# A new border between two stages: five comparisons for a recurrence, two projection banks, and constants made elsewhere

## What is computed

```python
xn = layernorm(x)
q, k, v = xn @ Wq.T, xn @ Wk.T, xn @ Wv.T           # 16 heads of 32
attn = softmax(q k^T * 512**-0.5) + bias[s - t]      # relative bias after softmax
s = layernorm(attn @ v) * gamma + beta
h = square(relu(xn @ W_fc.T))                        # 2048 wide
y = h @ W_proj.T
mem, count = 0, 0
for _ in range(5):                                   # leaky integrate and fire
    mem = 0.9 * mem + y - (mem > 1)
    count += (mem > 1)
out = x + s * silu(count / 5)
```

## Time and profile before

| | |
|---|---|
| median of three runs | 3676.3 us (3675.13 to 3678.26) |
| the profiled execution | 3674.0 us |
| span of the profiled execution | 3672.2 us |
| PE busy | 3474.0 us, 95% |
| DVE busy | 2733.0 us, 74% |
| ACT busy | 2623.7 us, 71% |
| POOL busy | 1575.7 us, 43% |
| DMA moved | 260.90 MB, mean 71 GB/s |

### The profile page before, as it was taken

One profiled execution on the slowest core, in us unless ns is written; L12 is line 12 of the kernel. 1 busy time (PEld: TensorE's weight loads), 2 busy tenths in 40 slices (PEclk: granted clock), 3 DMA queues, 4 the chain that ended last, 5 costly groups with the idle time before them and its releaser, 6 DMA issues.

```text
span 3672.2 us, 55309 instructions
## 1 busy us (share of the span) xinstructions
PE 3474.0 (95%) x20204; PEld 1475.0 (40%) x20204; DVE 2733.0 (74%) x4090; ACT 2623.7 (71%) x3917; POOL 1575.7 (43%) x898
## 2 busy tenths in 40 slices
PE   3999999999999998799999999999999999999985
PEld 1444444444444443334334343343343433434331
DVE  5366666666766667877787887887888888788786
ACT  4233333333333332799999999999999999999994
POOL 1000000000000000266777778677776777777867
PEclk6999999999999999899999999999999999999997
DMA  4011111111111111313223133232232222323221
GB/s 174 30 42 41 42 41 41 41 42 41 50 62 41 41 41 35 92 42 92 76 81 117 59 92 105 76 112 69 86 111 76 87 93 82 93 84 90 82 76 64
DMA packets 141405, 260.90 MB, mean 71 GB/s; under 512 B 19248, under 2 KB 52784, under 8 KB 140624
## 3 DMA queue, kind: packets, MB, share of 16 engines
q1 hardware_dynamic: 141136, 257.37, 22.1%
HBM read 155.77 MB, written 59.83 MB: 59 GB/s over the span
## 4 chain that ended last, share of the span: by engine, by line
ACT 36%; issue 10%; PE 7%; DVE 6%; POOL 1%; DMA 0%; ACTq 0%; SPq 0%; DVEq 0%; POOLq 0%
ACT recurrence_or_probs L1078 19%; ACT s_sb L1085 17%; DVE s_sb L1136 3%; PE misc L955 2%; PE acc L1030 2%; PE s_ps L999 2%; PE s_ps L1013 1%; DVE gate_or_tokens L1222 1%; POOL recurrence_or_probs L1329 1%; DVE nat L1170 1%; DMA xT<-xnT 0%; DVE outT L1155 0%; PE misc L938 0%; DVE recurrence_or_probs L90 0%; DVE frs L1212 0%
## 5 line engine op out<-in xcount | busy, mean ns | idle before, releaser
L1136 DVE TENSOR_SCALAR_CACHE_REDUCE s_sb<-s_ps 128x1024 f32<-128x1024 f32 x1024 | 1243.8, 1221 | 373.0 <-PE s_ps L999 338.6
L1329 POOL TENSOR_TENSOR recurrence_or_probs<-recurrence_or_probs,toep 128x2048 f32<-128x2048 f32 (+3 forms) x384 | 1321.6, 3461 | 275.6 <-ACT recurrence_or_probs L1078 275.6
L1085 ACT ACTIVATE s_sb<-s_sb,nmax 128x1024 f32<-128x1024 f32 x1024 | 1195.1, 1167 | 11.3 <-DVE s_sb L1136 11.1
L1078 ACT ACTIVATE recurrence_or_probs<-s_ps 128x1024 f32<-128x1024 f32 x1024 | 1058.7, 1035 | 16.8 <-PE s_ps L1013 16.6
L434 PE MATMUL ps_fc<-xnT_part,w_fc 128*128 128x512 f16 x3072 | 706.1, 380 | 1.4 <-DVE xnT_part L573 1.4
L447 PE MATMUL ps_y<-w_pr,hid_part 128*128 128x512 f16 x3072 | 704.5, 379 | 0.0
L514 ACT ACTIVATE relu<-ps_fc 128x512 f32<-128x512 f32 x256 | 152.8, 597 | 733.2 <-PE ps_fc L434 733.2
L999 PE MATMUL s_ps<-kst,qst 96*128 96x512 f16 x2048 | 613.9, 381 | 52.8 <-ACT recurrence_or_probs L1078 43.8
L1013 PE MATMUL s_ps<-qst,kst 99*128 99x512 f16 x2048 | 616.2, 383 | 2.4 <-DMA qst<-sub_rows 0.8
L1364 POOL MEMSET unit<- 128x16 f32 x1 | 0.1, 111 | 1408.3 <-POOLq L329 1408.3
L1030 PE MATMUL acc<-recurrence_or_probs,val 128*32 128x512 f32 x4096 | 547.4, 607 | 14.8 <-POOL recurrence_or_probs L1329 11.0
(11 more groups left out here) (117 smaller groups left out, 2537.6 us busy)
## 6 DMA issues: line engine op xcount, KB each, us to landing
toep<-table_rows SPq DMA_DIRECT2D x32, 2048.0 KB, 8.1
qst<-nat SPq DMA_DIRECT2D x384, 64.0 KB, 2.0
kst<-nat SPq DMA_DIRECT2D x384, 64.0 KB, 2.0
x_in<-in_x SPq DMA_DIRECT2D x16, 1024.0 KB, 7.4
xnT<-xnT_part SPq DMA_DIRECT2D x32, 512.0 KB, 4.2
gate<-gate_or_tokens SPq DMA_DIRECT2D x16, 1024.0 KB, 4.3
xT<-xnT SPq DMA_DIRECT2D x32, 512.0 KB, 9.2
x_or_gate<-gate SPq DMA_DIRECT2D x64, 256.0 KB, 2.8
```

Source lines behind the costliest of these rows:

```text
L1078: nc.scalar.activation(prob[:, k % PROBS, 2 * second:2 * second + 2, :].rearrange("p j n -> p (j n)"), s_ps[:, item_buffer(pair_item(m)), ...
L1085: nc.scalar.activation(s_sb[:, i % 4, :], s_sb[:, i % 4, :], ACT.Exp, bias=nmax[:, par, j, st:st + 1], scale=-1.0, accum_out=den[:, par, j ...
L1136: nc.vector.tensor_scalar(s_sb[:, i % 4, :], s_ps[:, item_buffer(tile_item(n)), :], -1.0, None, ALU.mult, ALU.min, accum_out=nmax[:, par, ...
L1329: nc.gpsimd.tensor_tensor(tile, tile, toep[:, par, :, at:at + width], ALU.add).then_inc(biased, 1)
```

## The change

- `SpikingGate`: the 13 operations of the recurrence become five comparisons with thresholds that the host finds by bisection (`count_spikes`). The bisection runs the recurrence in float32 for each y that it tries. In the first stage they are at steps 3 to 7 of the next chunk, the sigmoid at steps 8 to 10, the gate at step 13 of that same chunk, and SP stores it then. Only chunk 15 is left over the barrier.
- x of batch 0 (`xT_first`, 2 MB) is fetched by SP in chunk 4 of the first stage, into the part of `gate_or_tokens` that is free then. The first stage's end awaits it. The load of `xT` stays where it was.
- In the prelude, projections alternate between `misc` and the first half of the third buffer of `s_ps` (`prelude_bank`); ScalarE makes the high parts and takes v, VectorE only makes the low parts of q and k.
- `identh` is made by GpSimd with the weights, the ones in `kst` by GpSimd at the start of the second stage, and `consts` is awaited in `sum_values` and `rows`, where the constants are read; slot 0 awaits the ones.
- ScalarE's second load of the function tables goes.

```diff
@@ SpikingGate @@
+    def count_spikes(self, c, i):
...
+        wait(dve, self.lif, c * self.STEPS + i)
         if i == 0:
             dve.wait_ge(self.y_ready, c * 4 + 4)
...
+            op = self.nc.vector.tensor_scalar(self.spikes, self.y, self.thresholds[0], None, ALU.is_ge)
         else:
...
+            op = self.nc.vector.scalar_tensor_tensor(self.spikes, self.y, self.thresholds[i], self.spikes, ALU.is_ge, ALU.add)
         op.then_inc(self.lif, 1)
@@ prepare_weights @@
             pool.wait_ge(ident_step, 2)
+            nc.gpsimd.tensor_copy(w["identh"][:], w["ident"][:]).then_inc(ident_step, 1)
@@ feed_forward, sync @@
-                if not (isinstance(c, int) and c < 2):
-                    spiking.store(sp, c - 2)
+                if c == 4:
+                    sp.wait_ge(xt_stored, 64)
+                    for half in range(2):
+                        for part in range(2):
+                            sp.dma_start(spiking.xT_first[:, part, :, half * 512:(half + 1) * 512],
+                                         d["xnT"].rearrange("c a (k p) s -> c a p k s", p=P)[half, part]).then_inc(first_loaded, 16)
+                if c >= 1:
+                    spiking.store(sp, c - 1)
@@ feed_forward, scalar @@
-                    if f < 3 and not (isinstance(c, int) and c < 2):
-                        spiking.sigmoid(c - 2, f)
+                    if 8 <= f < 11 and not first:
+                        spiking.sigmoid(c - 1, f - 8)
@@ feed_forward, vector @@
-                    if f == 3 and not (isinstance(c, int) and c < 2):
-                        spiking.recurrence(c - 2, 13)
-                    if f >= 3 and not first:
-                        spiking.recurrence(c - 1, f - 3)
+                    if 3 <= f < 3 + STEPS and not first:
+                        spiking.count_spikes(c - 1, f - 3)
+                    if f == 13 and not first:
+                        spiking.gate_chunk(c - 1)
@@ attention @@
-CONSTS = 4 + TB - 1
...
+CONSTS = 2 + TB - 1
+
+LAST_SPIKES = {(-2, 3): 0, (-2, 9): 1, (-2, 15): 2, (-2, 19): 3, (-2, 23): 4}
...
+        def prelude_bank(n):
+
+            return (s_ps[:, RING - 1, :BANK], 1, spiking.xT_first) if n % 2 else (misc, 0, spiking.xT_first)
@@ attention, tensor @@
-            pe.wait_ge(consts, CONSTS)
             slots(pe, slot)
@@ attention, scalar @@
+            def prelude_takes(s, h):
...
+                    act.wait_ge(qk_ps, n + 1)
+                    nc.scalar.activation(nat[:, which, 0, c * 512:(c + 1) * 512], prelude_bank(u)[0][:], ACT.Copy,
+                                         scale=SCALE if which == 0 else 1.0).then_inc(qk_hi, 1)
...
-            load_exp_ln_tables(nc, act)
-            for i in range(3):
-                spiking.sigmoid(NC - 2, i)
@@ attention, vector @@
-            nc.vector.tensor_copy(identh[:], w["ident"][:]).then_inc(consts, 1)
-            nc.vector.memset(kst[ROWS:ROWS + SUBTRACTED], 1.0).then_inc(consts, 1)
...
-            spiking.recurrence(NC - 2, 13)
@@ attention, gpsimd @@
+            nc.gpsimd.memset(kst[ROWS:ROWS + SUBTRACTED], 1.0).then_inc(kst_ones, 1)
```

More of the change, by code:

```diff
@@ L11 @@
 from contextlib import ExitStack
+import numpy as np
 import concourse.bass as bass
@@ L32, with spike_thresholds, spikes @@
 TERMS = ((0, 0), (0, 1), (1, 0))
+def spike_thresholds():
+    f = np.float32
+    def spikes(y):
+        mem, count = f(0.0), 0
+        for _ in range(STEPS):
+            mem = f(f(f(f(BETA) * mem) + y) - f(1.0 if mem > f(1.0) else 0.0))
+            count += int(mem > f(1.0))
+        return count
+    found = []
+    for n in range(1, STEPS + 1):
+        low, high = f(0.0), f(2.0)
+        while np.nextafter(low, high) < high:
+            middle = f((low + high) / f(2.0))
+            low, high = (low, middle) if spikes(middle) >= n else (middle, high)
+        found.append(float(high))
+    return found
 def load_exp_ln_tables(nc, act):
@@ L937, in project_v @@
                     t = c * 4 + q
-                    last = nc.tensor.matmul(misc[:, q * P:(q + 1) * P], xT[:, a, k, t * P:(t + 1) * P],
+                    last = nc.tensor.matmul(bank[:, q * P:(q + 1) * P], x[:, a, k, t * P:(t + 1) * P],
                                             w["v"][:, bb, k, s.next_hg * P:(s.next_hg + 1) * P],
@@ L942, in project_v @@
                     last.then_inc(v_ps, 1)
-                    last_use[0] = (v_read, s.g * 2 + 2 + c + 1)
+                    last_use[spare] = (v_read, s.g * 2 + 2 + c + 1)
             def project_qk(s, u, part):
+                bank, spare, x = prelude_bank(u) if s.g < 0 else (misc, 0, xT)
                 if part == 0:
-                    take_misc()
-                    if u < 2 and s.ahead_hg == 0:
+                    take_misc(spare)
+                    if u < 2 and s.ahead_hg == 0 and s.main:
                         pe.wait_ge(xt_loaded[u], (s.b + 2) * 32)
@@ L1052, in slot @@
                 s = Slot(b, hg)
-                last_use[0] = ((tr_read, s.g * 2 - 1) if s.prev else (rows_read, 1) if s.main else (qk_read, 4) if s.scores else None)
+                if s.g == 0:
+                    pe.wait_ge(kst_ones, 1)
+                    pe.wait_ge(qk_read, 8)
                 for h in range(2 * SLOT_STEPS):
@@ L1103, in slot @@
                 for k in range(SLOT_STEPS):
-                    if isinstance(s.g, int) and s.g == -1 and 3 <= k < 6:
-                        spiking.sigmoid(NC - 1, k - 3)
                     if s.main:
@@ L1109, in slot @@
                         exp_sum(*s.tile_before(k))
+                    if s.g < 0:
+                        prelude_takes(s, 2 * k)
+                    if s.g == -2 and k >= SLOT_STEPS - 3:
+                        spiking.sigmoid(NC - 1, k - SLOT_STEPS + 3)
                     if k == 3 and s.main:
@@ L1248, in take_misc @@
                     take_values(s)
-                if h in VALUES and VALUES[h][1] and s.scores:
+                if h in VALUES and VALUES[h][1] and s.scores and s.main:
                     take_v(s, VALUES[h][0])
@@ L1270, in slot @@
                         copy_acc(s.g, s.par, 0)
[L1271 to L1273 removed]
+                    if (s.g, h) in LAST_SPIKES:
+                        spiking.count_spikes(NC - 1, LAST_SPIKES[s.g, h])
+                    if (s.g, h) == (-1, 15):
+                        spiking.gate_chunk(NC - 1)
                     if tiles:
```

98 lines of the change are left out of this document (52 added, 46 removed).

## The result

| | before | after |
|---|---|---|
| median, four runs each | 3677.28 us (3675.13 to 3679.47) | 3653.86 us (3653.07 to 3655.55) |
| the profiled execution | 3674.0 us | 3654.54 us |
| its span | 3672.2 us | 3652.8 us |

The ratio is 0.9937, 95% interval 0.992 to 0.9954: 23.4 us less by the medians, between 17 and 29 by the interval. What follows explains those 19.5, from the traces.

The account below looks back on a forecast made before the run. About 90 us around the border were taken as a serial chain, TensorE bounding the first stage; 24.0 (first score) + 0.4 (slot -1) = 24.4 us off 3676.3 gave 3651.9 us, range 3647.2 to 3658.5.

Parts of the forecast that it names:

- First stage, nothing: First stage: TensorE is the bound, so fewer VectorE operations and the moved sigmoid, gate store and x fetch change nothing.
- The wait for `far`: Start of slot -2: VectorE next waits for far, whose fourth DMA is issued at 1438.5 and lands at 1441.1.
- The ones on GpSimd: Slot -2: GpSimd's memset takes 6.88 to 12.8 us beside VectorE's comparisons and costs them 1.0.
- the row on L280: Earlier trace: two-input VectorE operations took 2.34 alone, up to 5.68 while GpSimd squared; read as 0.65 lost per us.
- my bounds: VectorE's loss beside GpSimd's memset of the ones: from nothing up to 2.0 to 5.9 us.
- VectorE decides slot -2: Slot -2: VectorE sets the pace, TensorE's projections are loose; low parts end at 1454.1, or 1455.1 with GpSimd's cost.
- The rival that put the half clock at the border: TensorE falls to 1.2 GHz at the border and bounds slot -2: gain 19.9, or 18.1 with late issue; chance 0.1.
- Stacking: Before the first score: the first head needs six DMAs, 5 x 0.63 + 2.0 = 5.2 us.
- First score: End of the border chain: first score at 1460.3 against 1484.31, 24.0 us gained, the main term.
- Slot -1: Slot -1: +2.9 us at full clock, -2.1 at half, about +0.4 with one of two places at half clock.
- the mean that I took: Slot -1: about +0.4 us taken, for one of the two places at half clock.
- the three later periods: Slot -1 after the tenth maximum: periods of four maxima go from 5.90 to 6.04 us each, 0.4 lost together.

Follow-up runs that it names:

- a2: Changed kernel with VectorE's wait for far moved from before its first comparison to slot 0; first score 24.80 us from the stage's start (25.07 in the changed kernel).
- c2: Changed kernel with extra unread matmuls in TensorE's gaps in slots -2 and -1; first score to first pair 39.11 us (44.36 in the changed kernel).

## Why the prediction was right, and where its steps were off

The forecast was 3651.9 us, the median 3653.9, in the range; the gain was put at 24.4 and the medians give 23.4. By the traces, which have 20.7 at the border, it was 3.7 too large, and that the medians come closer is in part luck of the scatter: two later sets of nine runs of the kernel before have medians of 3675.06 and 3676.40.

- **First stage, nothing**: right. TensorE's busy time did not move, with the sigmoid, the gate store and the fetch of x in their new places. The stage's start moved by 0.9 for another reason, above.
- **The wait for `far`**: right that VectorE waits for it next; I counted 4.0 us from the stage's start, and it was 4.8 to 5.3 in seven traces. In the changed kernel the last of the four landed 3.42 after its issue. The earlier trace rows give a median of 2.6, and I took it for the last; the longest in the trace of before was 3.1. Beside the memset this cost nothing, since the comparison ended at 8.17 whenever it began.
- **The ones on GpSimd**: this is the step that failed, and it makes up what the first score misses. The memset took 6.92, the lower bound. I put a cost of 1.0 on the two-input comparisons, at 0.65 per us of overlap, by the row on L280. Measured, the two-input ones lost nothing, and the one-input comparison, for which I had an end at 5.2 us from the stage's start (4.0 and 1.2), ended at 8.17: 3.0 in place of 1.0, of which 2.2 are its stretch and 0.8 went under the longer wait. The row on L280 shows a holding until GpSimd is done, and I read a rate out of it. That the cost stayed in my bounds is luck: the wait for `far` had let most of the memset pass, and in a2 the stretch alone is 6.1.
- **VectorE decides slot -2**: right for three of four low parts; the third waited 0.23 for TensorE at half clock. I had written that TensorE was loose there, and had looked at the 1.3 us of idling ahead of the first projection, not at the idling ahead of the third, which by my own times was over 2 us and was 5.8. The rival that put the half clock at the border was wrong on the place.
- **Stacking**: 5.2 predicted, 5.3 measured.
- **First score**: 24.0 predicted, 22.1 measured: the 2.0 of the ones.
- **Slot -1**: +0.4 predicted, -1.4 measured. To the second maximum it lost 0.3 (3.98 against 3.66), and from there to the tenth it gained 0.6 (15.14 against 15.72); for these two the mean that I took comes to +0.8. The larger miss is the three later periods, for which I had only -0.4 and no price for the clock: they took 7.36, 6.04 and 5.91 against 5.90 each, a loss of 1.6, nearly all of it in the first, where the second half of u = 1 was at half clock. At full clock the working holds: I had 40.0 between first score and pair (42.92 less 2.9), c2 gave 39.1, with 13.03 to the tenth maximum (12.9 worked out) and later periods of 5.91. That moving the high parts to ScalarE is worth nothing there was right, 0.2 us.

## What to carry to other kernels

A chain at the border of two stages is worth more than busy time in a stage that another engine bounds: 250 us of VectorE's work went for nothing, 8 operations on the chain for 9.6. Where two waits stand one behind the other, or one lies beside the other, taking away one shows little (1.1 and 0.3 us at the first score) and both show 6.4; so when a wait is removed, ask what is next, and try both. Look for what a helper engine's new work runs beside, instruction by instruction, and at each gap that an edit leaves on TensorE: an earlier start that is followed by idling can be paid in the clock (the third projection took 4.50 behind 5.78 of idling, 2.76 with the gap filled).

## What the runs showed of the hardware that I had not expected

- A float32 tensor_scalar of 128x2048 in SBUF (1.22 us alone) that began beside a GpSimd memset of 3 partitions by 8192 float16 ended 1.1 us after the memset, whenever it began: 7.28 us in a2, 3.38 in the changed kernel. A scalar_tensor_tensor of the same shape took 2.29 beside the same memset.
- It seems to go the other way too. In the stage of the weights GpSimd's rounding of the 128x128 identity, put beside VectorE's L301, took 2.35 us and ended at 31.30, 0.16 after the operation of VectorE that ran beside it (to 31.14). No run has this rounding on GpSimd alone; on VectorE it took 0.16 before the change. First the timeline of the changed kernel, then that line of before:

```profile
25.46 5.68 DVE L301 SCALAR_TENSOR_TENSOR w_fc<-stage_fc,work,w_fc 128x2048 f16<-128x2048 f32 x1
28.95 2.35 POOL L211 CAST identh<-ident 128x128 f16<-128x128 f32 x1
```

```profile
1437.75 0.16 DVE L1289 CAST identh<-ident 128x128 f16<-128x128 f32 x1
```

- Matmuls whose result is not read, put into TensorE's gaps (the longest had been 5.78 us), kept the granted clock at 1.00 through a stretch in which it had been 0.86 and 0.75.
